# Attention weights and values of a graph layer as high and low f32r parts, rows passed through DRAM, and the weighting in seven pieces

## What is computed

```python
q, k, v = x @ wq + bq, x @ wk + bk, x @ wv + bv
scores = sum(q[dst] * k[src], -1) * scale + edge_weight * we + be
exp_s  = exp(scores - segment_max(scores, dst)[dst])
attn   = exp_s / max(segment_sum(exp_s, dst)[dst], 1e-12)
out    = segment_sum(v[src] * attn[:, None], dst)
x = layer_norm(x + out + (x @ ws + bs), g1, b1)       # "the skip rows": x + x @ ws
x = layer_norm(x + gelu(x @ w1 + b1f) @ w2 + b2f, g2, b2)
```

## Time and profile before

| | |
|---|---|
| Median of 3 runs | 1742.78 us (1741.48 to 1746.64) |
| The profiled execution | 1748.1 us |
| Its span, first to last instruction | 1746.4 us |
| Busy share: PE, PEld, DVE, ACT, POOL | 94%, 78%, 69%, 54%, 14% |

### The profile page before, as it was taken

The page is one execution under the profiler, slowest core; times in us unless marked ns, Lnnn a source line. Parts: engine busy times, 40 slices in busy tenths (PEclk is TensorE's granted clock), DMA queues, the critical chain, the costliest instruction groups (busy, mean ns, idle before and its releaser), DMA issues.

```text
span 1746.4 us, 41845 instructions
## 1 busy us (share of the span) xinstructions
PE 1633.9 (94%) x11388; PEld 1365.2 (78%) x11388; DVE 1203.4 (69%) x3373; ACT 944.2 (54%) x2928; POOL 251.6 (14%) x315
## 2 busy tenths in 40 slices
PE   6989999999799999999989999999999997993887
PEld 5978888888588888888778888888888887992554
DVE  6838998988589899889855555555555546988232
ACT  4757888888588888888723333333333333550111
POOL 0050000000000000000010011111111001772574
PEclk9998999999899999999999999999999998995797
DMA  8162333333433333333432222111111240111773
GB/s 190 63 153 81 94 95 94 93 94 94 138 92 95 94 93 94 94 94 94 108 67 79 80 79 79 74 72 70 71 72 77 76 110 1 54 61 47 222 230 94
DMA packets 213042, 164.29 MB, mean 94 GB/s; under 512 B 38054, under 2 KB 204915, under 8 KB 209578
## 3 DMA queue, kind: packets, MB, share of 16 engines
q1 hardware_dynamic: 182048, 96.78, 21.0%
q0 software_dynamic: 16544, 57.40, 9.6%
q10 hardware_dynamic: 14400, 9.55, 1.9%
HBM read 82.34 MB, written 85.50 MB: 96 GB/s over the span
## 4 chain that ended last, share of the span: by engine, by line
PE 83%; DVE 5%; DMA 4%; issue 3%; POOL 2%; ACT 2%; SPq 1%; ACTq 0%; POOLq 0%; DVEq 0%
PE bank L1431 31%; PE bank L1464 16%; PE bank L1452 13%; PE bank L1416 9%; PE bank L1471 3%; PE bank L1496 2%; PE bank L1504 2%; DMA arena<-rows_dram,arena 1%; POOL out L695 1%; DMA adj<-arena 1%; PE bank L1360 1%; SPq L500 1%; ACT arena L812 1%; PE bank L1562 1%; PE bank L1565 1%
## 5 line engine op out<-in xcount | busy, mean ns | idle before, releaser
L786 ACT ACTIVATE arena<-bank,tables 128x128 f32<-128x128 f32 x2048 | 585.2, 369 | 152.0 <-PE bank L1416 151.9
L1431 PE MATMUL bank<-arena 128*125 128x128 f32 x4096 | 588.4, 287 | 12.7 <-DVE arena L1076 12.7
L1431 PEld LDWEIGHTS bank<-arena 128*125 128x125 f32 x4096 | 490.6, 189 | 66.3 <-DVE arena L1076 13.1
L1076 DVE TENSOR_TENSOR arena<-iota_row,tables 128x250 f32<-128x250 f32 x1024 | 422.3, 413 | 6.3 <-DMA term_rows<-arena 6.2
L1102 DVE SCALAR_TENSOR_TENSOR arena<-arena,tables,bank 125x128 f32<-125x128 f32 x1023 | 352.7, 345 | 90.6 <-PE bank L1431 41.3
L1464 PE MATMUL bank<-V,arena 125*125 125x256 f32 x1250 | 297.2, 383 | 5.9 <-ACT arena L812 5.9
L812 ACT COPY arena<-bank 125x500 f32<-125x500 f32 (+1 forms) x175 | 90.7, 533 | 380.6 <-PE bank L1471 380.6
L1464 PEld LDWEIGHTS bank<-V,arena 125*125 125x125 f32 x1250 | 223.8, 189 | 38.3 <-ACT arena L812 10.6
L1143 DVE CUSTOM_DVE_ANT_0 arena<-arena 125x3200 f32<-125x3200 f32 x25 | 87.3, 3493 | 222.6 <-ACT arena L795 222.6
L640 POOL COPY gidx<-arow 125x1 uint32 (+1 forms) x25 | 36.4, 1457 | 1193.4 <-DVE wk_sb L1143 859.3
L1416 PE MATMUL bank<-dist_rhs,arena 5*128 5x128 bf16 x2048 | 202.2, 218 | 6.2 <-DMA arena<-term_rows 5.3
(11 more groups left out here) (234 smaller groups left out, 1523.8 us busy)
## 6 DMA issues: line engine op xcount, KB each, us to landing
adj<-arena SPq DMA_DIRECT2D x512, 125.0 KB
q_dram<-arena ACTq DMA_DIRECT2D x25, 125.0 KB, 2.2
wq_sb<-q_dram SPq DMA_DIRECT2D x25, 125.0 KB, 8.0
rows_dram<-tables SPq DMA_DIRECT2D x25, 125.0 KB
rows_dram<-x SPq DMA_DIRECT2D x25, 125.0 KB
V<-in_x SPq DMA_DIRECT2D x5, 560.0 KB
tables<-in_x SPq DMA_DIRECT2D x5, 560.0 KB
V<-w_dram SPq DMA_DIRECT2D x40, 65.3 KB
```

Source lines behind the costliest of these rows:

```text
L786: ins = nc.scalar.activation(Ys[:, q, k, :], bank[2 + s][:, k * LO:(k + 1) * LO], ACT.Relu, scale=nval_tab[:, bass.ds(i, 1)])
L1076: ins = V_.tensor_tensor(Xs[:, s, cols, :], iota_row[:, 0:TILE].unsqueeze(1).to_broadcast([P, SUB, TILE]), code_tab[:, bass.ds(g * GC + k ...
L1431: ins = mm(o, Xs[:, j % STAGES, k, :], Ys[:, j % STAGES, k, :], start=(k % SUB == 0), stop=(k % SUB == SUB - 1))
```

## The change

- **Parts of V and of the weights.** V is split once into `v_parts` (low and high, f32r). The high part is copied by ScalarE in five pieces before the first exponentials, the low part made by VectorE's `value_rest` at the start of the first `weigh`. For each group of transposed weights ScalarE's copy now writes `p_hi` (f32r), and VectorE's `weight_rest` makes `p_lo` from the same bank. For each of the 25 blocks TensorE multiplies `p_hi` with both parts of V at once (512 columns, low products in the left half of the bank, high ones in the right) and `p_lo` with the high part (256 columns, right half). VectorE's `back` adds both halves, one addition more.
- **Weighting in seven pieces.** `weigh` runs piece by piece, each behind its exponentials, with a partial sum each and a small reduction in `back`. TensorE's transposes wait for the piece they need. VectorE's order is a new one: the low parts of tile t and the weighting of tile t+1 in turns (`mix`), then the mask, then `back`.
- **Skip rows and finished rows through DRAM.** The skip rows no longer stay in SBUF: they are stored with each tile's Q (the row of `q_dram` is 256 wider), and SP loads each tile's back in attention (`load_skip`). Finished rows of the first 23 tiles go out to `y_dram` (`store_y`) and come back behind the last scores, ahead of x, into `x1`, which now lies over the K buffer. GpSimd clears the pad of the new row buffer once, at the start.
- **Statistics** of the first 23 tiles stand one turn earlier in `pipeline`'s count (with `back`'s lag of 2: behind the `back` of tile 22, ahead of the scores of tile 24).
- **Row numbers on TensorE.** `wcnt` is spread over the partitions by five small products with a selection matrix that VectorE makes (`pick`), at a new pause before pair 10; `counts` moves to pair 11. The store and the five loads on SP are gone.
- Two lists of semaphores are merged into one (`slot_in`), to keep their number down.

The core of the diff:

```diff
-        SPREAD_AT, COUNTS_AT = 4, 10
+        SPREAD_AT, ROWS_AT, COUNTS_AT = 4, 10, 11
+        Y_PARTS = ((0, 5), (5, 14), (14, NT - 2))
+        V_PARTS = [slice(i * NT // 5 * D, (i + 1) * NT // 5 * D) for i in range(5)]
...
 SP
-            sp.wait_ge(last_set, 1)
-            sp.dma_start(last_lin..., wrow[0:TILE, :]).then_inc(last_stored, 16)
-            for b in range(WIN):
-                sp.dma_start(arow0[b:TILE:WIN, :], spread, ...).then_inc(last_in, 16)
...
-            with sp.Fori(2, NT // 2) as i:
-                load_q(2 * i, 0, i)
-                load_q(2 * i + 1, 1, i)
+            for t in range(NT - 2):
+                load_skip(t + 2)
+                store_y(t)
+                if t + 5 < NT:
+                    load_q(t + 5, (t + 5) % 2, (t + 5) // 2)
...
 ACT
+            for c in V_PARTS:
+                nc.scalar.copy(v_parts[0:TILE, 1, c], V_buf[0:TILE, c]).then_inc(k_hi_set, 1)
-                    nc.scalar.copy(PT[0:TILE, s, j:j + n, :], ...
+                    nc.scalar.copy(p_hi[0:TILE, (s + g) % 2, 0:n, :], ...
...
 DVE
-            def weigh(t, s, u):
-                dve.wait_ge(e_ready, t + 1)
-                V_.tensor_tensor_reduce(out=Z[0:TILE, s, :], in0=Z[0:TILE, s, :], in1=A_sb[0:TILE, s, :], ...)
+            def weigh(t, s, b):
+                c, n = SCH[b]
+                dve.wait_ge(e_ready, len(SCH) * t + b + 1)
+                V_.tensor_tensor_reduce(out=Z[0:TILE, s, c:c + n], in0=Z[0:TILE, s, c:c + n], in1=A_sb[0:TILE, s, c:c + n], ...)
+            def weight_rest(t, s, g):
+                dve.wait_ge(pt_ready, len(TRG) * t + g + 1)
+                V_.tensor_tensor(p_lo[...], bank[4 + g % 2][...], p_hi[...].bitcast(F32), ALU.subtract).then_inc(p_split, 1)
...
+            def mix(t, s, u):
+                LAG = 2
+                for g in range(len(TRG)):
+                    weight_rest(t, s, g)
+                    if g >= LAG and not (isinstance(t, int) and t + 1 >= NT):
+                        weigh(t + 1, 1 - s, g - LAG)
...
-                if isinstance(t, int) and t == NT - 1:
+                if isinstance(t, int) and t == NT - 3:
                     statistics(st1, 0, NT - 2)
-            pipeline(dve, (guard, 1), (back, 3), (early_statistics, 2), (later_query_rest, 0), (weigh, 1), (exclude, 0))
+            pipeline(dve, (guard, 1), (first_weigh, 1), (mix, 2), (exclude, 0), (back, 2), (early_statistics, 2))
...
 PE
-                        ins = mm(bank[6 + s][0:TILE, 0:D], PT[0:TILE, s, j, :], V[:, j, :], ...)
+                        whole = (bank[6 + s][0:TILE, 0:2 * D], p_hi[0:TILE, slot, j - j0, :], v_parts[0:TILE, :, c])
+                        rest = (bank[6 + s][0:TILE, D:2 * D], p_lo[0:TILE, slot, j - j0, :], v_parts[0:TILE, 1, c])
```

More of the change, by code:

```diff
@@ L231, in gnn_moe @@
         RT = NT * NEXP
-        k_flat = kT[:, :, :, :].rearrange("p k j l -> p (k j l)")
-        lg, work, hot32, total, upto, fresh = (k_flat[:, i * RT:(i + 1) * RT] for i in range(6))
+        lg, work, hot32, total, upto, fresh = (late[:, i * RT:(i + 1) * RT] for i in range(6))
         hot = hot32.bitcast(BF16)[:, 0:RT]
@@ L527, in _ @@
                 load_q(t, t, 0)
+                load_skip(t)
             def put(g, j, i):
@@ new lines, in mix @@
+            def mix(t, s, u):
[4 more added lines that the diff above has]
+                        weigh(t + 1, 1 - s, g - LAG)
+                    if g == LAG and not (isinstance(t, int) and t + 2 >= NT):
+                        query_rest(t + 2, s, u + 1)
+                if not (isinstance(t, int) and t + 1 >= NT):
+                    for b in range(len(SCH) - LAG, len(SCH)):
+                        weigh(t + 1, 1 - s, b)
@@ L1146, in back, with first_weigh @@
+            def first_weigh(t, s, u):
+                if isinstance(t, int) and t == 0:
+                    for i in range(len(V_PARTS)):
+                        value_rest(i)
+                    for b in range(len(SCH)):
+                        weigh(0, 0, b)
             def back(t, s, u):
+                late_tile = isinstance(t, int) and t >= NT - 2
                 b_ord.begin(t)
-                dve.wait_ge(p_ready, t + 1)
+                dve.wait_ge(p_ready, len(SCH) * (t + 1))
+                b_ord(V_.tensor_reduce(den[:, s:s + 1], den_parts[:, s, :], AX, ALU.add))
@@ L1375, in spread, with row_numbers @@
                 mm(bank[1][:, 0:4 * PP], ones[0:PP, :], e_diag, start=True, stop=True).then_inc(rows_bc, 1)
+            def row_numbers():
+                pe.wait_ge(last_set, 1)
+                for q in range(WIN):
+                    ins = mm(bank[0][0:TILE, q * NWB:(q + 1) * NWB], pick[:, q, :], wcnt[0:TILE, :], start=True, stop=True)
+                ins.then_inc(spread_ps, 1)
             def counts():
                 pe.wait_ge(diag_set, 3)
+                pe.wait_ge(arow_set, 1)
                 for q in range(0, SBLK, 4):
```

161 lines of the change are left out of this document (105 added, 56 removed).

## The result

The change makes the kernel slower, by a little: 1750.36 us (median of 20 runs, 1740.90 to 1757.47) against 1739.34 us of before (20 runs, 1734.73 to 1746.64), a ratio of 1.0052 with a 95% interval of 1.0037 to 1.0067 (estimated over all executions; the quotient of the two medians is 1.0063). The same kernel in another set gave 1.0033 (1.0008 to 1.0058). The forecast, 1737 us with a range of 1719 to 1768, has the time in its range and the sign wrong. The three runs of before that were shown ahead of the prediction (1741.48 to 1746.64) lie in the upper half of the 20, and its profiled execution (1748.1) was above them all.

What follows compares the result with a forecast made beforehand. The prediction took TensorE as the bound in attention, with VectorE close behind at the next tile's scores. Its terms, -6.4 + 3.5 + 4.5 + 2.7 - 2.1 - 2.6 - 5.2 = -5.6 us, gave 1737 us, range 1719 to 1768.

Steps and rivals of the forecast that it cites:

- The products: V part of each attention tile: a pair of products takes 0.352 us instead of 0.432, 2.0 us less TensorE work.
- The first wait of a tile: Start of each tile's V part: TensorE starts at 1.97 us instead of 1.32 after the first transpose, 0.65 lost.
- VectorE's row: End of each attention tile: back part ends at 18.57 us, fifth score piece starts at 19.43 instead of 18.39, 1.04 lost.
- VectorE's row longer by 0.5 us: Rival, each attention tile: a semaphore wait per piece or GpSimd's gather issue adds 0.5 us; +12, 1749 us, chance 0.13.
- The start and the end of attention: Start: 3.5 us added; end: 4.5 added for the statistics, 2.7 for low clock, 2.1 saved in the last tile.
- The row numbers: Before the products: their stage starts at 124.0 instead of 126.64, saving 2.6 us; the clock stays up, saving 5.2.
- the rival of a clock that falls all the same: Start of the products: the clock falls despite the shorter idle, 5.2 us comes back, 1742 us; chance 0.12.
- The 1.7 us that the prediction puts on the adds beside GpSimd's clearing: Before the products: without a port lock between VectorE's adds and GpSimd's memset, the product stage would start 1.7 us earlier.
- The clock inside a tile: Rival, attention tiles: two idle stretches of about 1.0 us lower the clock in every tile; 1781 or 1759 us, chance 0.12.
- The sum: Whole kernel: -6.4 for the tiles, +3.5 +4.5 +2.7 -2.1 for attention's start and end, -2.6 -5.2 for row numbers: -5.6 us.

Runs made afterwards that it cites:

- unroll: The kernel after with VectorE's attention loop written out; 1771.36 us, ratio 1.0019 to the kernel before.
- rownum: The kernel before with only the change's row-number part; 1739.99 us, ratio 0.9997 to before, and run again 1738.91 us, 0.9995.
- after_again: The kernel after, unchanged, measured and profiled a second time; 1745.65 us, ratio 1.0033 to the kernel before.
- before_again: The kernel before, unchanged, measured and profiled a second time on the slower chip; 1769.68 us, ratio 1.0003.
- memset_late: The kernel after with GpSimd's clearing of the ones rows put behind VectorE's eight code adds; 1748.96 us in one execution, no ratio.

## Why the prediction was wrong

**The products: right.** A pair is 0.35, the value taken, and the scores begin 12.87 after the first transpose, as forecast.

**The first wait of a tile: right.** 0.7 us more, 2.02 after the first transpose.

**VectorE's row: the step that failed.** Its work was forecast within 0.4 us: `back` ends 18.17 after the first transpose in the tiles written out and 18.40 to 18.46 in the loop, against 18.57. I took the first score piece to follow at once, and the fifth on TensorE 0.86 later, 19.43; the sum has no term for the branch of VectorE's loop and none for its computed waits. In the tiles written out it came at 19.25, and the tile took 22.76, even a little less than 22.82. In the loop it came at 19.61 and 20.05 in turn. The experiment unroll shows that this difference is the loop. By the rows, a semaphore wait whose value the loop computes adds some 0.1 us (`back` loses 0.23 to 0.29 in three of them), and the branch 0.5. Before, VectorE ran the same kind of loop, with 0.24 us behind its branch, and the tiles were 23.07 and 23.10 in turn: it waited 8.91 us in each tile. When the change took that idle time away, the loop's cost came to light. I read the durations and gaps of instructions in the trace, but never asked whether VectorE's own control flow lay on the path. The mean of the 22 ordinary tiles is 23.22 (22.82 forecast, 23.07 before): +3.3 us instead of -6.4.

This was one of the rivals, VectorE's row longer by 0.5 us, with 1749 us and a chance of 0.13. Its size was about right (0.40 a tile) and the causes named for it were not: no gap shows between the weighting pieces, and GpSimd's gather is there in the first tiles too. That its 1749 us lie so near the 1750.36 measured is luck: it still holds the 7.8 us of the row numbers, which did not come, and a start and end of attention that were priced too dear.

**The start and the end of attention: right in kind, priced 1 to 4 us too dear.** TensorE's idle time before the fifth piece of tile 1, and at tiles 24 and last:

```profile
888.25 0.79 PE L1535 MATMUL bank<-k_hi,q_hi 128*125 128x512 f32 x1 [8.89 <-DVE wk_sb L1166]
...
1427.96 0.79 PE L1535 MATMUL bank<-k_hi,q_hi 128*125 128x512 f32 x1 [5.22 <-DVE wk_sb L1166]
...
1450.07 0.50 PE L1551 MATMUL bank<-v_parts,p_hi 125*125 125x512 f32 x1 [3.41 <-DVE p_lo L1185]
```

From the first scores to the row at 888.25 it is 3.25 more than before (forecast 3.5), of which 1.9 is left at the first transposes. The rest is the clock of before's profile: from this row to the first transposes it is 6.3 us there, 4.9 in rownum and 5.0 in after; against rownum, 3.3 is left. The stall at tile 24 is 5.2 (forecast 5.5), and with the low clock behind it the interval is 5.6 longer, 7.0 in after_again (forecast 7.2). The last tile is 2.6 shorter, 2.1 against rownum (forecast 2.1). With the tiles' 3.3 that makes the 8.2 us of the table (10.2 against rownum), where 2.2 had been forecast.

**The row numbers: half wrong.** The first product at 124.4 instead of 126.6 is as forecast (124.0):

```profile
124.40 0.60 PE L1499 MATMUL bank<-dist_rhs,arena 5*128 5x128 bf16 x8 [0.89 <-issue]
```

The stretch behind it, which was at 0.50 in the earlier trace rows:

```profile
131.00:139.00 8.00, 8.00 (x72) 6.76 (x71) 7.22 (x24) 6.70 (x24) 0.00 (x0) 1.00 0.34 98
```

In this profile its clock is 1.00, but 0.79 over 125 to 133; in after_again it was 0.86, with 0.59 over 125 to 133. So the rival of a clock that falls all the same came true in part. How deep it falls belongs to the execution: from the first product to the 321st record of the products' line (1431 in before, 1514 in after) it is 63.25 us in before and 60.85 in before_again, 59.30 and 60.85 in the two profiles of after, 59.30 and 60.83 in the two of rownum. The part alone brought -0.5 and -0.9 us by the measured ratios, and the intervals reach down to -3.1 and -4.3, where I had counted -7.8. The step that failed is that I priced a wait and a clock drop from one execution as if each had them. The 1.7 us that the prediction puts on the adds beside GpSimd's clearing did not show either: in memset_late the product stage comes no earlier.

**The clock inside a tile: right.** Two idle stretches of about a microsecond a tile don't bring it down (1.00 over the tiles).

**The sum.** Attention +8.2 instead of +2.2, the row numbers about -1 instead of -7.8: +7, between the two measured ratios (+5.8 and +9.0 us), instead of -5.6. So two steps failed, not one: the tiles took 9.7 us more than forecast, of which the start and the end gave back 4 against before's profile, and the row numbers brought 7 less.

## What to carry to other kernels

When a change takes the idle time out of an engine that was not the bound, price its control flow too: the branch of its loop and the waits with computed values, at the place in the row where they lie. A loop's body is not free to grow: here twice the tiles in it cost some ten times as much at the branch. And don't price a wait or a clock drop from one profile where a second profile of the same kernel can tell whether it comes each time. If an engine becomes the gate while its busy share is under 80%, look at what stands ahead of the released work in its order and move that to where the engine waits anyway; here that, with V's low part staged, turned a loss of 0.3 to 0.5% into a gain of 1.8 to 1.9%.

## What the runs showed of the hardware

- The branch back of VectorE's loop added about 0.5 us to its row with a body of two tiles and 4.0 to 5.9 us with one of four, with no releaser in the trace; the sequencer's next instruction came 0.26 and 3.7 to 5.6 us behind the branch.
- An f32r product of 256 columns between two of 512 takes 0.11 to 0.12 us of TensorE's row at the clock of 1.00, half of one of 512 columns.
- VectorE's 128x256 additions (0.35 us each) and GpSimd's clearing of 2x8192 in bf16 (6.9 us): an add that met the clearing ended only with it. Two adds took 6.34 beside it, 0.70 apart from it. The other way round wasn't seen.
- One chip took 27 to 29 us more than others for the kernel before (1768.19 against 1739.34 to 1741.18), 8 of them by the profiles ahead of the products, where TensorE stood idle six times for 0.8 to 2.5 us with nothing to wait for, and 14 to 24 in the experts' stage. What part of it is the chip and what the execution, the runs don't say.
